# Six of eight batches take their first layer norm by features, with mean and 1/deviation fetched through DRAM as rows

## The reference, cut to what matters

```
n1  = (x - mean(x)) / sqrt(var(x) + 1e-5)          # per token, over the 256 features
s   = n1 @ ctx.T                                   # scores, 256 tokens x 120
x   = x + (gelu_tanh(s) * s) @ ctx
n2  = (x - mean(x)) / sqrt(var(x) + 1e-5)
h   = silu(n2 @ w1.T * s1) * (n2 @ w2.T * s2)      # 1024 wide
h   = gelu(h @ h1.T * t1); h = gelu(h @ h2.T * t2) # 1024 x 1024 each
out = x + h @ w3.T * s3
```

## Time and profile before

| | |
|---|---|
| median of 3 runs | 323.46 us (323.4 to 323.8) |
| the profiled execution, its own time | 323.3 us |
| its span (first to last instruction) | 321.5 us |
| TensorE busy | 314.1 us, 98% |
| VectorE busy | 265.1 us, 82% |
| ScalarE busy | 220.7 us, 69% |
| GpSimd busy | 59.4 us, 18% |
| granted TensorE clock, mean | 1.00 |

### The profile page before, as it was taken

The page is one execution under the profiler, slowest core; times in us unless marked ns, Lnnn a source line. Parts: engine busy times, 40 slices in busy tenths (PEclk is TensorE's granted clock), DMA queues, the critical chain, the costliest instruction groups (busy, mean ns, idle before and its releaser), DMA issues.

```text
span 321.5 us, 4932 instructions
## 1 busy us (share of the span) xinstructions
PE 314.1 (98%) x1628; PEld 227.2 (71%) x1628; DVE 265.1 (82%) x502; ACT 220.7 (69%) x369; POOL 59.4 (18%) x96
## 2 busy tenths in 40 slices
PE   8899999999999999999999999999999999999994
PEld 5799768774756667577898866876574756657693
DVE  4786996898896999998789494499899998998494
ACT  3557857783887857869825565978588975968740
POOL 5365010311110114114030003001121110220000
PEclk9999999999999999999999999999999999999999
DMA  6799999999999989998417055347599977877003
GB/s 209 255 206 252 207 261 304 345 340 405 323 341 418 295 301 250 331 258 203 137 66 261 3 196 194 135 130 260 197 282 278 415 236 296 206 188 196 0 34 107
DMA packets 31615, 74.91 MB, mean 233 GB/s; under 512 B 2145, under 2 KB 14177, under 8 KB 29025
## 3 DMA queue, kind: packets, MB, share of 16 engines
q0 software_dynamic: 21840, 52.43, 58.0%
q1 hardware_dynamic: 9744, 22.11, 20.1%
HBM read 71.39 MB, written 6.29 MB: 242 GB/s over the span
## 4 chain that ended last, share of the span: by engine, by line
PE 96%; DVE 1%; DMA 1%; ACT 0%; POOL 0%; issue 0%; DVEq 0%; POOLq 0%
PE P L1397 32%; PE P L1391 30%; PE P L1349 18%; PE P L1483 5%; PE P L1470 4%; PE P L1313 2%; PE P L1321 2%; PE P L1305 2%; DMA xs<-in_x 1%; PE P L1559 0%; POOL rs L465 0%; PE P L1552 0%; ACT xt L599 0%; DVE st L876 0%; PE P L1545 0%
## 5 line engine op out<-in xcount | busy, mean ns | idle before, releaser
L1397 PE MATMUL P<-TL,WR 128*128 128x512 f32 x448 | 107.3, 396 | 0.0
L1391 PE MATMUL P<-TH,WB 128*128 128x512 f16 x448 | 99.8, 379 | 0.0
L1397 PEld LDWEIGHTS P<-TL,WR 128*128 128x128 f32 x448 | 84.0, 188 | 18.4
L651 ACT ACTIVATE TH<-H 128x512 f16<-128x512 f32 x112 | 67.9, 624 | 22.3 <-DVE H L967 14.0
L1391 PEld LDWEIGHTS P<-TH,WB 128*128 128x128 bf16 x448 | 42.4, 98 | 53.1 <-issue 4.5
L974 DVE TENSOR_TENSOR TL<-H,TH 128x512 fp32r<-128x512 f32 x112 | 73.3, 684 | 7.0 <-ACT TH L651 4.4
L1349 PE MATMUL P<-X,W 128*128 128x512 f32 (+1 forms) x320 | 62.5, 351 | 0.0
L1349 PEld LDWEIGHTS P<-X,W 128*128 128x128 f32 x320 | 51.7, 189 | 7.6
L967 DVE TENSOR_TENSOR H<-H 128x512 f32<-128x512 f32 x64 | 41.8, 682 | 0.0
L945 DVE SCALAR_TENSOR_TENSOR H<-P,sc,SLY 128x512 f32<-128x512 f32 (+1 forms) x40 | 25.3, 637 | 18.2 <-PE P L1349 10.4
L672 ACT ACTIVATE H<-P 128x512 f32<-128x512 f32 x48 | 28.5, 594 | 13.4 <-DMA blocks_h<-H 5.1
(11 more groups left out here) (88 smaller groups left out, 257.5 us busy)
## 6 DMA issues: line engine op xcount, KB each, us to landing
WR<-blocks_h POOLq DMA_DIRECT2D x16, 1024.0 KB, 6.0
WR<-in_h POOLq DMA_DIRECT2D x11, 1024.0 KB, 8.9
WB<-blocks_h POOLq DMA_DIRECT2D x16, 512.0 KB, 5.3
WB<-in_h POOLq DMA_DIRECT2D x12, 512.0 KB, 7.2
H<-in_h POOLq DMA_DIRECT2D x8, 512.0 KB, 15.2
blocks_h<-H SPq DMA_DIRECT2D x4, 1024.0 KB, 8.2
SLY<-in_h SPq DMA_DIRECT2D x8, 512.0 KB, 5.1
SLY<-in_w SPq DMA_DIRECT2D x6, 512.0 KB, 7.6
```

What stands on the lines that cost most here:

```text
L651: eng.activation(TH[:, f % RING, :], operand(c, L, s, kk), ACT.Copy).then_inc(s_hi, 1)
L1391: return eng.matmul(bank(c, L, s, m)[:, :], WB[r % WRING][:, at:at + 128], TH[:, fill(c, L, s, kk) % RING, :], start=(not lower_first and ...
L1397: return eng.matmul(bank(c, L, s, m)[:, :], WR[r % WRING][:, at:at + 128], TL[:, fill(c, L, s, kk) % RING, :], start=(lower_first and s in ...
```

## The change

Batches 2 to 7 (`b >= ROWS`, with `ROWS = 2`) no longer turn their first norm.

- x also comes laid out by features (`x_feat`), 256 KB for each of the six batches. `load_feat(b)` puts it into `xn[0]`, which is free of its old use.
- `rstd(0, b)` writes 1/deviation beside the mean in `mv`, so a token has the pair (mean, 1/deviation). `row_out(b)` stores the 128 x 2 pairs to DRAM, 8 bytes each; `row_in(b)` loads them back as one row of 512 numbers into each of the 128 partitions of `xt`, 256 KB. Both are issued by SP and stand in its order; `row_in` waits for its `row_out` to have landed.
- `centre(b)` on DVE takes the row of means from the features (128 x 512). `score(b)` reads that. `scores_scaled(b)` on DVE multiplies the scores by the row of 1/deviation on the way out of the bank (120 x 256, into `hh`). `act_s` and `gate` now read `hh`.
- Gone for these batches: `scale(0, b)` (DVE), `turn(0, b)` (PE), `copy_t(b)` (ACT).
- Places: `score(2)` goes from group 2 to group 11, `score(3)` from group 14 to group 15 of the second pass of `layer1(0)`; `score(4)` and `score(5)` come before the lower pass of k = 0 to 3 instead of after it; `score(6)` and `score(7)` stand after groups 6 and 8 of `layer1(2)`, where their turns were.

```diff
@@ SP @@
+            def load_feat(b):
+                if b < ROWS + 2:
+                    eng.wait_ge(s_tr[0], b - 1)
+                else:
+                    eng.wait_ge(s_s, b - 1)
+                eng.dma_start(feat(b), x_feat[:, b - ROWS, :, :]).then_inc(s_xf[b - ROWS], 16)
+            def row_out(b):
+                eng.wait_ge(s_rs[0], b + 1)
+                eng.dma_start(rows[b - ROWS].rearrange("j p v -> p j v"), mv[:, 0, b % 4, :, :]).then_inc(s_row[b - ROWS], 16)
+            def row_in(b):
+                if b < ROWS + 2:
+                    eng.wait_ge(s_s, b - 1)
+                else:
+                    eng.wait_ge(s_sr, b - ROWS - 1)
+                eng.wait_ge(s_row[b - ROWS], 16)
+                eng.dma_start(xt[:, b % 2, :, :].rearrange("p c t -> p (c t)"),
+                              rows[b - ROWS:b - ROWS + 1].rearrange("b j p v -> b (j p v)").broadcast_to([128, 2 * TB])).then_inc(s_rb[b - ROWS], 16)
...
             eng.wait_ge(s_w12[1], 16)
+            load_feat(2)
+            row_out(2)
             load_cf(1)
+            load_feat(3)
+            row_in(2)
             load_ct(1)
+            row_out(3)
+            row_in(3)
             for p in range(4):
                 sums_out(p)
...
-            for i in range(2, 9):
+            load_feat(4)
+            load_feat(5)
+            for i in range(2, 6):
                 load_check(i)
+            row_out(4)
+            load_check(6)
+            row_in(4)
+            row_out(5)
+            load_check(7)
+            row_in(5)
+            load_check(8)
+            load_feat(6)
+            load_feat(7)
+            for b in (6, 7):
+                row_out(b)
+            for b in (6, 7):
+                row_in(b)
@@ ACT @@
             def act_s(b):
-                eng.wait_ge(s_s, b + 1)
+                if b >= ROWS:
+                    eng.wait_ge(s_sr, b - ROWS + 1)
+                    scores = hh[:, b % 2, :]
+                else:
+                    eng.wait_ge(s_s, b + 1)
+                    scores = side(b)[0:S, 0:TB]
@@ DVE @@
+            def centre(b):
+                eng.wait_ge(s_xf[b - ROWS], 16)
+                eng.wait_ge(s_rb[b - ROWS], 16)
+                mean = row(b, 0).rearrange("p (c t) -> p c t", c=1).broadcast_to([128, 2, TB])
+                eng.tensor_tensor(feat(b), feat(b), mean, ALU.subtract).then_inc(s_cen, 1)
+            def scores_scaled(b):
+                eng.wait_ge(s_s, b + 1)
+                eng.wait_ge(s_o, b - 1)
+                eng.tensor_tensor(hh[:, b % 2, :], side(b)[0:S, 0:TB], row(b, 1)[0:S, :], ALU.mult).then_inc(s_sr, 1)
...
-            if t == 0 and m == 1:
-                scale(0, 3)
+            if t == 0 and m == 3:
+                centre(2)
+            if t == 0 and m == 6:
+                centre(3)
+            if t == 0 and m == 7:
+                scores_scaled(2)
             if t == 2 and m < 2:
-                scale(0, 6 + m)
+                centre(6 + m)
@@ PE @@
             def score(b):
...
+                    eng.wait_ge(s_cen, b - ROWS + 1)
+                    tokens = feat(b)
             def attend(t, i):
-                if (t, i) == (0, 2):
+                if (t, i) == (0, 11):
                     score(2)
-                if (t, i) == (0, 8):
-                    turn(0, 3)
-                if (t, i) == (0, 14):
+                if (t, i) == (0, 15):
                     score(3)
                 if t == 2 and i in (6, 8):
-                    turn(0, 3 + i // 2)
-                if t == 2 and i in (12, 14):
-                    score(i // 2)
+                    score(3 + i // 2)
```

More of the change, by code:

```diff
@@ L124, in xattn_ffn @@
         wS = {n: nc.dram_tensor(f"blocks_{n}", [len(STORED), 128, 4, 512], bf16, kind="Internal").ap() for n in ("h1", "h2")}
+        rows = nc.dram_tensor("rows", [NB - ROWS, 2, 128, 2], f32, kind="Internal").ap()
         P = [ctx.enter_context(nc.psum_tensor(f"P{i}", [128, 512], f32)) for i in range(8)]
@@ L149, in xattn_ffn @@
         s_tr = [sem("s_tr1"), sem("s_tr2")]
+        s_xf = [sem(f"s_xf{b}") for b in range(ROWS, NB)]
+        s_row = [sem(f"s_row{b}") for b in range(ROWS, NB)]
+        s_rb = [sem(f"s_rb{b}") for b in range(ROWS, NB)]
+        s_cen, s_sr = sem("s_cen"), sem("s_sr")
         s_xt, s_gl, s_X0 = sem("s_xt"), sem("s_gl"), sem("s_X0")
@@ L167, in xattn_ffn, with feat, row @@
         out_v = out.rearrange("(b p j) d -> b p j d", j=2, p=128)
+        def feat(b):
+            return xn[0][:, b % 2, :, :]
+        def row(b, v):
+            return xt[:, b % 2, :, :].rearrange("p c t -> p (c t)").rearrange("p (t v) -> p t v", v=2)[:, :, v]
         def side(b):
@@ L459, in rstd @@
                 eng.wait_ge(s_mv[norm], b + 1)
-                eng.tensor_tensor(rs[:, norm, b % 4, :], mv[:, norm, b % 4, :, 1], mhalf[:, :], ALU.pow).then_inc(s_rs[norm], 1)
+                to = mv[:, 0, b % 4, :, 1] if norm == 0 and b >= ROWS else rs[:, norm, b % 4, :]
+                eng.tensor_tensor(to, mv[:, norm, b % 4, :, 1], mhalf[:, :], ALU.pow).then_inc(s_rs[norm], 1)
             def rstd_half(norm, j):
@@ L806, in _ @@
                     hi4(c, 1, 4 + i)
-                    if i >= 2:
-                        if c == 0:
-                            copy_t(2 + i)
-                        else:
-                            gelu(c, 1, (1, 0), i)
+                    if i >= 2 and c == 1:
+                        gelu(c, 1, (1, 0), i)
                 if c == 0:
@@ L917, in gate @@
                     eng.wait_ge(s_o, b - 1)
-                eng.tensor_tensor(hh[:, b % 2, :], side(b)[0:S, 0:TB], gl[:, b % 2, :], ALU.mult).then_inc(s_h, 1)
+                scores = hh[:, b % 2, :] if b >= ROWS else side(b)[0:S, 0:TB]
+                eng.tensor_tensor(hh[:, b % 2, :], scores, gl[:, b % 2, :], ALU.mult).then_inc(s_h, 1)
+            def centre(b):
[7 more added lines that the diff above has]
+                eng.tensor_tensor(hh[:, b % 2, :], side(b)[0:S, 0:TB], row(b, 1)[0:S, :], ALU.mult).then_inc(s_sr, 1)
             def resid(b):
@@ L1047, in square @@
                             test(n)
-                    if c == 0 and s == 3:
-                        scale(0, 4)
                     if s in (4, 5):
@@ L1059, in square @@
                         stats(0, 6)
+                        centre(4)
                     if c == 0 and s == 5:
-                        scale(0, 5)
+                        centre(5)
                     if s == 6:
@@ L1101, in early_products @@
                 b = 4 * c + 2
+                if c == 0:
+                    scores_scaled(3)
                 gate(b)
@@ L1166, in layer1 @@
                         scale(1, 1)
-                    if m == 2:
-                        scale(0, 2)
                     if m == 4:
@@ L1174, in layer1 @@
                     both(t, m)
-                    if t == 0 and m == 1:
-                        scale(0, 3)
+                    if t == 0 and m == 3:
[4 more added lines that the diff above has]
+                        scores_scaled(2)
                     if t == 2 and m < 2:
-                        scale(0, 6 + m)
+                        centre(6 + m)
+                    if t == 2 and m in (5, 6):
+                        scores_scaled(1 + m)
                     if t % 2 == 1 and 2 <= m <= 5:
@@ L1224, in _ @@
                     lo4(c, 1, k)
+                    if c == 0 and k == 5:
+                        scores_scaled(4)
+                        scores_scaled(5)
                 if c == 0:
@@ L1295, in turn @@
                     eng.wait_ge(s_X1, b - 1)
-                if norm == 0 and b in (4, 5):
-                    gelu_done(eng, 0, 1, b, 0)
                 for j in range(2):
@@ L1310, in score @@
                 eng.wait_ge(s_cf[b // 2], 16)
-                eng.wait_ge(s_xt, b + 1)
+                if b >= ROWS:
+                    eng.wait_ge(s_X1, b - 1)
+                    if b in (4, 5):
+                        gelu_done(eng, 0, 1, b, 0)
+                    eng.wait_ge(s_cen, b - ROWS + 1)
+                    tokens = feat(b)
+                else:
+                    eng.wait_ge(s_xt, b + 1)
+                    tokens = xt[:, b % 2, :, :]
                 for c in range(2):
-                    out_ = eng.matmul(side(b)[0:S, 0:TB], cf[:, (b // 2) % 2, b % 2, c, :], xt[:, b % 2, c, :],
+                    out_ = eng.matmul(side(b)[0:S, 0:TB], cf[:, (b // 2) % 2, b % 2, c, :], tokens[:, c, :],
                                       start=(c == 0), stop=(c == 1))
@@ L1532, in layer1 @@
                             turn(1, 1)
-                        if i == 12:
-                            turn(0, 2)
                 eng.wait_ge(s_X1, 2 * t + 2)
```

18 lines of the change are left out of this document (6 added, 12 removed).

## The result

The changed kernel takes 343.4 us (median of 4 runs, 342.0 to 344.4) where the kernel before, run on the same chip, takes 323.6 (323.4 to 323.8). The ratio is 1.061, with an interval of 1.056 to 1.066. It is slower, as forecast, but by 19.8 us and not by 2.9, far above the range given, which ended at 329.6.

A forecast was written before the change was run, and what follows sets the result against it. PE was taken to bound the kernel: 4.4 us late at batch 3's rows, less 1.5 gained at batches 4 to 7, gave +2.9, or 326.3 us (0.9% slower). Own range 324.5 to 328; with rivals, 322.6 to 329.6.

The forecast's parts named there:

- What bounds the kernel, and one for one: Whole kernel: PE, busy 314.1 of 321.5 us, bounds it; work removed or waits added there count one for one.
- What goes: Batches 2 to 7: six times four transposes leave PE, 2.2 us in sum, 0.7 in the first 31 us.
- rival (d): DVE: `centre` and `scores_scaled` cost twice the estimate and PE waits at each batch, 326 us; chance 0.02.
- `row_in(2)`, whose chain starts eight us earlier, [...] lands well before `centre(2)` wants it: Batch 2's rows: chain starts before POOL's transfers fill the engines, so no wait was counted for it.
- 5.2 us for `row_out(3)`: Batch 3's store, issued at 24.0: lands after 5.2 us, with bounds of 2.0 and 9.6.
- 5.2 for `row_in(3)`: Batch 3's row load behind its store: 5.2 us under load, landing at 34.4.
- The sum of the term: Batch 3's new DMAs: `row_in(3)` lands at 34.4, product 0 starts at 35.9 instead of 31.59, 4.3 us late.
- Rival (c), the clock: Around 30 us: PE's wait lowers its clock for product 0's upper pass, middle 2.7 us, total 329.0; chance 0.30.
- "The other batches", −1.5: Batches 4 to 7: DMAs land in time, 1.5 us gained, bounds 1.0 and 1.8.
- "if a batch behind makes PE wait": Sign of being wrong: PE waiting at a later batch; no wait above 0.3 us was expected at batches 4 to 7.
- Rival (a): Batch 3's rows come in time, `row_in(3)` landing by about 29 to 30, total 322.2 us; chance 0.14.

The follow-up runs named there:

- Experiment 11: Kernel before with only batches 6 and 7 coming by features (`ROWS = 6`), 2 to 5 turned as before: 322.89 us, ratio 0.9979.
- Experiment 5: Changed kernel with the stores of batches 2 and 3 in 16 pieces of 128 bytes of other data instead of 256 of 8: 333.85 us, ratio 1.030.
- experiment 7: Changed kernel with the row DMAs of batches 2 and 3 ahead of the context load, batch 2's 1/deviation earlier on GpSimd: 337.74 us, ratio 1.042.
- experiment 4: Changed kernel with 60 matmuls of zeros on PE ahead of `score(2)` and of `score(3)`, to hold the clock up: 340.48 us, ratio 1.0511.
- experiment 1: Changed kernel with batches 2 and 3 turned as before, so batches 4 to 7 alone by features (`ROWS = 4`): 325.33 us, ratio 1.0065.
- experiment 8: The kernel of experiment 1 without its row stores, `row_in` reading 2 KB of x instead: 323.36 us, ratio 0.999.
- experiment 12: Changed kernel, all six batches by features, with no row store at all, every `row_in` reading x: 324.65 us, ratio 1.0032.
- experiment 6: Changed kernel with GpSimd's raw weight loads held back until `row_in(3)` has landed, batch 3's 1/deviation first: 338.66 us, ratio 1.047.
- experiment 9: Kernel before with two added 2 KB stores that nobody waits for, each in 256 pieces of 8 bytes: 327.06 us, ratio 1.0107.
- experiment 10: Kernel before with two added 2 KB stores that nobody waits for, each in 16 pieces of 128 bytes: 323.63 us, ratio 0.9999.
- experiment 3: Changed kernel with the rows of batches 2 and 3 loaded early from x, without a store before them: 326.6 us, ratio 1.0062.

## Why the prediction was right or wrong

**What bounds the kernel, and one for one: right.** But for half a microsecond the whole loss sits in PE's waits and in the clock behind them, and no wait was made up for later.

**What goes: right.** Experiment 11 gives 0.70 us for two batches, the 0.7 that I had read from the earlier trace rows. `centre` (0.68) and `scores_scaled` (0.42) cost what the earlier trace rows said; rival (d) fell. Its own sum was off as well: 323.46 - 2.2 + 3.3 is 324.6 and not 326.

**"`row_in(2)`, whose chain starts eight us earlier, [...] lands well before `centre(2)` wants it": wrong.** This is the step that failed first: a wait put at nothing, and without a sum. The chain started at 17.9, six us earlier than batch 3's and not eight, its two DMAs took 6.8 and 9.3, and it landed at 34.1, 7.5 us late. Had I put my own 5.2 + 5.2 onto it, I would have had 28.3 against a place at about 26, and seen that batch 2 waits as well. And since both pairs stand in SP's order, batch 3's store could not go before batch 2's had landed and the context load was issued: 27.35, not 24.0. That batch 2's rows are "out of SP's way by then" was the sentence that hid this.

**5.2 us for `row_out(3)`: wrong by 7.1.** I valued the store by its bytes and by the wait before the first byte, and noted its 256 pieces only in passing, as if that were the packets of the 512 KB load at 127.3; that load has 144 in the trace of before, and 9.6 was my upper bound. It took 12.3. Experiment 5 puts 9.5 us of the total on the pieces of the two stores, experiment 7 5.7 us on the order of issue (the two overlap). 5.2 for `row_in(3)` was near: 5.9.

The sum of the term: 3.35 for the later issue, 7.1 for the store and 0.7 for the load make 11.2, by which `row_in(3)` landed after my 34.4. From there to the start of product 0 I had 1.5 us and the trace 2.75, at the lower clock. 4.3 + 11.2 + 1.25 = 16.8.

**Rival (c), the clock: right in kind.** I gave it 0.30 and 2.7 us, and it cost 2 to 3 (experiment 4). That the size fits is luck: I had put all of it on the upper pass of product 0 behind one wait of 5 us, and the trace has 1.25 there and 0.9 in the scores of batch 3, behind two waits of 7.5 and 6.0. By the Trainium skill (TensorE: Matmul & The Clock Gate, "Part 1: The HAM clock gate") the clock falls to half in a pause and comes back under work. The trace agrees: 0.50 from 35.0 to 40.5, 1.00 after 53.2.

**"The other batches", −1.5: wrong in sign.** "Delayed by at most the packets of a 256 KB load" looked at SP's own transfers alone. The weight loads of POOL for which PE waits at 99 and 142 us had no slack to give, and a store in small pieces costs them far more than its 2 KB. Measured by itself the term is +1.7 (experiment 1) instead of −1.5: 2.0 go with the stores (experiment 8), and of the 1.2 that remain 0.8 are one wait for a weight load. In the changed kernel's own profile it comes to about nothing, 1.6 of waits against 1.5 of turns. My sign of being wrong, "if a batch behind makes PE wait", came true here.

**Where the 19.8 us are**, by the ladder of medians: 343.4 as changed; 333.9 without the 8-byte pieces of batches 2 and 3 (−9.5); 326.6 with their rows not waiting for a store at all (−7.3); 324.7 without the stores of batches 4 to 7 (−2.0); 321.4 is what the turns alone would give (323.6 − 2.2), which leaves 3.3. The first two steps are far beyond the noise. The third is not clear of it here (ratios of 1.0038 to 1.0085 and 1.0011 to 1.0053) and rests on experiments 1 and 8, where the same step has the same size. The rest is what the added transfers and operations cost in some way, not measured one by one: in the execution profiled in experiment 12, waits for `WR<-in_h` (0.6), for the second norm (1.6) and for `centre` (0.4) make 2.6 of the 3.3. The clock's 2 to 3 us are within the first two steps.

Rival (a) leaned on the Trainium skill's fixed part of about 2.0 us for a DMA, counted as nearly constant (DMA: Bandwidth & Descriptors, "Anatomy of one DMA"). The section gives it for DMAs that GpSimd issues, while these are SP's. The quiet load of 240 KB in the earlier trace rows, 2.5 us in all, is in line with it; the quiet `row_in(3)` of experiment 6 is not, with 2.2 us before its first packet and 4.1 in all. Beside other transfers it holds still less: 3.9, 6.8, 8.2 and 12.3 us for 2 KB. The same page of the Trainium skill ("Specifications") has transfers below 512 bytes done as a read, a change and a write. That rule spoke against this change, and I had not weighed it. The pair of experiments 9 and 10 agrees only in part, because pieces of 128 bytes are below that size too and cost nothing that could be measured; the runs differ in the number of pieces as well, 16 against 256, and in the partitions that they leave from, 16 against 128.

## What to carry to other kernels

Count the pieces of a DMA, not its bytes: in the execution profiled in experiment 9, 2 KB in 256 pieces delayed the 1 MB load beside it by 6 us, though nothing waited for the store itself. A wait of about 3 us in TensorE's order then costs more than its length, since the matmuls behind it run at the lower clock. When a store and a load that depends on it enter an in-order queue, write down the issue and landing of each DMA in that order, for every batch, before trusting that the first pair is early. And place such pairs where no transfer beside them is due: the same change that loses 20 us over six batches gains 0.7 in the two whose transfers fall into such a stretch.

## What the runs showed of the hardware

- Beside a store of 2 KB in 8-byte pieces the DMA engines moved less than half, which their busy share hardly showed: 140 against 321 GB/s at 0.97 and 1.22 (experiment 9, 125 to 129 us, the second store; the first, at 115 us, cost no rate).
- The time of the program was less certain with them: 326.4 to 330.3 with the two added stores, 323.4 to 323.9 with the same bytes in larger pieces. They are not the only thing that does this: experiment 12, without any, spreads from 323.0 to 327.0.
- After a wait of TensorE of 2.7 or 3.0 us the matmuls behind it ran at the lower clock (16 in 5.52 and in 6.66 us, with 0.50 granted for 3 and 6 us), after one of 1.6 they did not (16 in 3.92). These are the profiled executions of experiments 3, 9 and 1.
- Issuing can hold SP up: it spent 2.13 us on the issue of one 256 KB load and 1.12 us on that of 2 KB, where 0.3 to 0.4 is usual in the same timeline. This too went with the pieces: with the store in 128-byte pieces (experiment 5) the same two took 0.60 and 0.33.
- A 256 KB load issued into idle DMA engines moved nothing for 2.2 us, and landed after 4.1 (experiment 6); in experiment 11 nothing moved for 2.0 us behind the issue at 159.96.
